# Half of a strip's candidate fetches ahead of a wait, half behind a store, in the last five rounds of GpSimd

## The chip, the cores and the metric

The kernel runs on one core of one Trainium2 chip. The metric is the device time of one execution in microseconds (us), the median of several runs.

## What is computed

Two graph layers on 8192 nodes with 64 features, with one dense weighted adjacency matrix `adj` (8192 x 8192, fp32, 268 MB):

```python
h = jnp.maximum(_layernorm(x, axis=-1), 0.0)
x = x + _L0_gnn_ref(h, L0_gnn_t, adj, L0_gnn_B, L0_gnn_W1, L0_gnn_b1, L0_gnn_W2, L0_gnn_b2)
h = jnp.maximum(_layernorm(x, axis=-1), 0.0)
x = x + _L1_gnn_ref(h, adj, L1_gnn_W, L1_gnn_att_self, L1_gnn_att_neigh, L1_gnn_bias)
return x
```

Layer 0 is `tanh([h, t] @ W1 + b1) @ W2 + b2` plus `Wt @ XB - rowsum(Wt) * XB` with `Wt = adj` and `XB = h @ B.T`. Layer 1 is an attention whose scores get `-1e10 * (1 - adj)`: where one entry of a row of `adj` leads the others by enough, the softmax picks that neighbour alone, and the layer's output is one gathered row, `relu(feats[best] + bias)`. The kernel computes that case, proves for its inputs that it holds, and keeps a general path behind a branch that isn't taken here.

## The kernel before, in words

The rows of `adj` are worked on in 16 strips of 512. A strip is 8 chunks of 2 MB (`adj_t`, a transposed copy) that SyncE loads into `ring`, a ring of four slots. On each chunk TensorE makes the products (L1034) and row sums (L1042, L1052), ScalarE casts it to fp16 (L546), and VectorE takes running maxima (L744) and adds pairs (L733). TensorE, VectorE and ScalarE run the strips in a loop. The small work on strip s-1 and s-2 is woven in.

The search for the strongest neighbour goes in steps over three strips. VectorE finds for each row the two best classes of 64 columns and writes their addresses into `cls_row` (L775). GpSimd, whose code is the function of L381, then fetches those two classes of 64 entries for 4 x 128 rows: eight indirect DMAs into `cand` (`fetch_rows`, L444 to L450). One strip later VectorE picks the largest (L788 to L800) and writes `best`. ScalarE writes the layer-1 features of a strip, with bias and relu, into `agg` (L579), and GpSimd stores them to `agg_dram` (`store_agg`, L439 to L442). When enough strips are stored, GpSimd gathers for each node the features of its best neighbour, 128 rows an indirect DMA, into `gathered` (`gather`, L457 to L464).

GpSimd's instructions stand in one order, written out by hand. In strips 1 to 10 a loop adds the bias b2 (L436), stores the features of strip s-1 and fetches the candidates of strip s. From strip 11 on come five rounds (L474 to L486), one for each entry of `WINDOWS` (L57). I call them rounds 0 to 4; they know the features of strips below 11, 12, 13, 14 and 15. Each of rounds 0 to 3 adds b2, waits for the gathers of the round before (`got`), stores the features, fetches eight times, waits until the stores landed (`agg_stored`), and gathers 14 times. Round 4 fetches four times and gathers four times.

Behind the rounds (L487 on) stand the last four fetches, eight late gathers (L492) that wait for the store of the last strip's features (`agg_last`, issued by SyncE at L337), two gathers, four scatter-adds into `out` (L501), two gathers, and four scatter-adds. SyncE stores the bulk of `out` after VectorE's additions (L920).

Of the kernel before, what the change touches and what calls it, by code (L numbers as in the profile page):

```python
# [35 lines left out]
S = N // W  # L36
TB = W // P
# [24 lines left out]
def build(nc, x, adj, adj_t, w1, w1_t, b1, t_in, w2, b2, b_t, w_gat, w_gat_t, att_self, att_neigh, bias, out):  # L62
    with ExitStack() as ctx:
# [6 lines left out]
        def sem(name):  # L70
            return ctx.enter_context(nc.semaphore(name))
# [157 lines left out]
        cls_row_done = sem("cls_row_done")  # L229
# [151 lines left out]
        def _(pool):  # L381
# [52 lines left out]
            def add_b2(s):  # L434
                x1 = x_tq[:, bass.ds(s * TB, TB), :]
                pool.tensor_tensor(x1, x1, b2_row[:, :].unsqueeze(1).to_broadcast([P, TB, D]),  # L436
                                   ALU.add).then_inc(x_b2_done, 1)

            def store_agg(s):  # L439

                pool.wait_ge(agg_ready, s + 1)
                pool.dma_start(agg_by_q[:, bass.ds(s, 1), :].rearrange("q a f -> q (a f)"), agg[:, :]).then_inc(agg_stored, 16)  # L442

            def fetch_rows(k0, k1):  # L444
                for k in range(k0, k1):
                    for g in range(CLS):
                        pool.indirect_dma_start(  # L447
                            out=cand[:, k, g * NB:(g + 1) * NB], out_offset=None, in_=classes,
                            in_offset=bass.IndirectOffsetOnAxis(ap=cls_row[:, k, g:g + 1], axis=0),
                        ).then_inc(cand_in, 16)  # L450

            def fetch_candidates(s):
                pool.wait_ge(cls_row_done, s + 1)
                pool.sem_inc(pool_past, 1)
                fetch_rows(0, TB)

            def gather(w, t0, t1):  # L457

                pool.wait_ge(best_done, (t1 + TB - 1) // TB)
                for t in range(t0, t1):  # L460
                    pool.indirect_dma_start(  # L461
                        out=gathered[:, t, :], out_offset=None, in_=agg_dram,
                        in_offset=bass.IndirectOffsetOnAxis(ap=best[:, t:t + 1], axis=0),
                    ).then_inc(got[w], 16)  # L464

            add_b2(0)
            fetch_candidates(0)
            add_b2(1)
            n0 = WINDOWS[0][0]
            with pool.Fori(1, n0) as s:  # L470
                add_b2(s + 1)
                store_agg(s - 1)
                fetch_candidates(s)
            for w, (known, t0, t1) in enumerate(WINDOWS):  # L474
                if known + 1 < S:
                    add_b2(known + 1)
                if w:
                    pool.wait_ge(got[w - 1], 16 * (WINDOWS[w - 1][2] - WINDOWS[w - 1][1]))
                store_agg(known - 1)
                if known < S - 1:  # L480
                    fetch_candidates(known)
                else:
                    pool.wait_ge(cls_row_done, S)
                    fetch_rows(0, TB // 2)
                pool.wait_ge(agg_stored, 16 * known)
                gather(w, t0, t1)  # L486
            fetch_rows(TB // 2, TB)  # L487
# [529 lines left out]
        def _(pe):  # L1017
# [47 lines left out]
            def turn_sums(s):  # L1065


                pe.wait_ge(rows_copied, s + 1)
                pe.wait_ge(acc_copied, s + 1)
                pe.wait_ge(hid_done, s + 1)  # L1070

                halves = [(k, slice(half, half + D), slice(k * P + half, k * P + half + D))
                          for k in range(TB) for half in (0, D)]
                for k, to, at in halves:
                    pe.matmul(ps_acc[to, k, D:2 * D], row_sb[:, at], fold_rows[:, :], start=True, stop=True)  # L1075
                for k in range(TB):
                    for _, to, at in halves[2 * k:2 * k + 2]:
                        pe.matmul(ps_acc[to, k, 0:D], acc_sb[:, at], b_t_twice[:, :], start=True, stop=False)
                    for _, to, at in halves[2 * k:2 * k + 2]:
                        pe.matmul(ps_acc[to, k, 0:D], hidden[:, at], w2_sb[:, :], start=False, stop=True)  # L1080
                for m in range(2):
                    last = pe.matmul(ps_xb[:, 2 * m:2 * m + 2, :].rearrange("q k d -> q (k d)"),  # L1082
                                     h_strip[:, m * P:(m + 1) * P], b_t_diag[:, :], start=True, stop=True)
                last.then_inc(acc_turned, 1)
# [155 lines left out]
```

## Time and profile before

| what | value |
|---|---|
| median of 3 runs | 794.06 us (792.35 to 794.34) |
| the profiled execution's own time | 793.22 us |
| its span, first to last instruction | 791.5 us |
| TensorE, VectorE, ScalarE, GpSimd busy | 86%, 82%, 75%, 49% |
| mean granted TensorE clock | 0.949 of full speed |

All numbers below are of that one profiled execution; the 1.7 us between its span and its time lie outside the instructions. A busy share is an average over the span: TensorE works until about 714 us, GpSimd until 783 us.

### The profile page before, as it was taken

What the parts mean: (1) busy time and instruction counts of PE and PEld (TensorE: products, weight loads), DVE (VectorE), ACT (ScalarE), POOL (GpSimd) and SP (SyncE); (2) the same over time, 40 slices, a digit from 0 to 9 for tenths busy, and PEclk for the clock granted to TensorE, in tenths of its full rate; (3) what the DMA queues carried; (4) which work ended last, traced back from release to release, by engine and by line L of the source; (5) the groups of instructions that cost most, each with busy time, mean ns of one, the idle gap of its engine ahead of it and who ended that gap; (6) DMA issues with size and microseconds to landing.
All of it is one profiled execution on the core that took longest, in us unless ns stands there. A gap on an engine that the chain in (4) does not pass through costs nothing.

```text
span 791.5 us, 13172 instructions
## 1 busy us (share of the span) xinstructions
PE 682.6 (86%) x4470; PEld 244.2 (31%) x4470; DVE 652.8 (82%) x944; ACT 594.0 (75%) x507; POOL 390.2 (49%) x281
## 2 busy tenths in 40 slices
PE   3999999999999999999999999999999999981100
PEld 1233333333333332333333333333333333330000
DVE  4586899989999999999898999999998989782420
ACT  3789888897889887888888888979888888770200
POOL 7000544435160808061533426170886878867774
PEclk9999999999999999999999999999999999995555
DMA  8999899999999999999999999999999999931151
GB/s 331 415 418 430 347 426 392 426 391 417 391 411 431 388 431 377 431 379 428 384 429 378 426 390 426 405 406 428 388 413 407 424 383 427 397 126 26 55 108 20
DMA packets 34544, 287.02 MB, mean 363 GB/s; under 512 B 7456, under 2 KB 13968, under 8 KB 18016
## 3 DMA queue, kind: packets, MB, share of 16 engines
q1 hardware_dynamic: 23168, 275.00, 83.9%
q0 software_dynamic: 9056, 9.73, 4.6%
q10 hardware_dynamic: 2304, 2.10, 0.8%
q8 instruction: 7, 0.11, 0.1%
q14 instruction: 9, 0.07, 0.0%
HBM read 279.46 MB, written 7.34 MB: 362 GB/s over the span
## 4 chain that ended last, share of the span: by engine, by line
PE 29%; DMA 22%; POOL 17%; issue 14%; DVE 13%; ACT 3%; DVEq 1%; SPq 0%; POOLq 0%; ACTq 0%
DMA ring<-in_adj_t 21%; PE acc L1034 18%; POOL gathered L461 7%; POOL cand L447 6%; DVE work L744 4%; PE row_sums L1042 4%; DVE work L733 4%; PE row_sums L1052 3%; ACT work L546 2%; POOL out L501 2%; DVE work L740 1%; POOL work L492 1%; PE ps_xb L1082 1%; DVE work L750 1%; PE ps_acc L1075 1%
## 5 line engine op out<-in xcount | busy, mean ns | idle before, releaser
L546 ACT CAST work<-ring 128x4096 f16<-128x4096 f32 x128 | 458.7, 3603 | 60.4 <-DMA ring<-in_adj_t 21.0
L1034 PE MATMUL acc<-ring,x_pb 128*64 128x512 f32 x2048 | 455.4, 596 | 13.7 <-DMA ring<-in_adj_t 13.5
L447 POOL DMA_INDIRECT cand<-in_adj,cls_row x128 | 231.8, 1811 | 64.8 <-issue 38.4
L744 DVE TENSOR_TENSOR work<-work 128x4096 f16<-128x4096 f16 x96 | 219.9, 2291 | 22.5 <-ACT work L546 19.5
L1034 PEld LDWEIGHTS acc<-ring,x_pb 128*64 128x64 f32 x2048 | 140.3, 137 | 316.3 <-issue 278.8
L733 DVE TENSOR_TENSOR work<-ring 128x2048 f32<-128x2048 f32 x90 | 210.4, 2352 | 7.1 <-DMA ring<-in_adj_t 5.0
L442 POOL DMA_DIRECT2D agg_dram<-agg x15 | 9.0, 600 | 258.0 <-ACT agg L579 200.8
L461 POOL DMA_INDIRECT gathered<-agg_dram,best x64 | 84.6, 1322 | 19.5 <-issue 19.5
L1052 PE MATMUL row_sums<-work,ones_cols 128*32 128x512 f32 x720 | 89.5, 598 | 0.1
L1042 PE MATMUL row_sums<-ring,ones_cols 128*32 128x512 f32 x608 | 72.4, 614 | 14.1 <-DMA ring<-in_adj_t 14.1
L436 POOL TENSOR_TENSOR x_tq<-x_tq,b_row 128x256 f32 (+1 forms) x16 | 29.5, 1846 | 42.7 <-DMA x_tq<-in_x 42.4
L740 DVE TENSOR_TENSOR work<-work 128x4096 f16<-128x4096 f16 x16 | 36.5, 2284 | 1.7 <-ACT work L546 1.7
L1042 PEld LDWEIGHTS row_sums<-ring,ones_cols 128*32 128x32 f32 x608 | 19.4, 112 | 57.3 <-issue 54.0
L1052 PEld LDWEIGHTS row_sums<-work,ones_cols 128*32 128x32 f32 x720 | 18.7, 109 | 54.2 <-issue 54.1
L617 ACT ACTIVATE tmp<-cen 128x64 f32<-128x64 f32 x64 | 15.6, 244 | 21.6 <-DVE cen L821 14.8
L604 ACT COPY acc_tq<-ps_acc 128x260 f32<-128x260 f32 x16 | 5.9, 370 | 28.3 <-remote 27.1
L1097 PE MATMUL ps_hid<-ident,h 128*128 128x128 f32 x2 | 0.7, 434 | 28.3 <-issue 28.3
L788 DVE MAX8 top_cand<-cand 128x8 f32<-128x128 f32 x64 | 13.8, 276 | 12.3 <-DMA cand<-in_adj,cls_row 12.3
L750 DVE TENSOR_TENSOR work<-work 128x2048 f16<-128x2048 f16 x16 | 19.6, 1225 | 2.3
L564 ACT ACT_TABLE_LOAD x16 | 20.5, 1283 | 0.3
L619 ACT ACT_TABLE_LOAD x16 | 20.5, 1283 | 0.3
L808 DVE TENSOR_TENSOR tmp<-ps_xb,acc_tq 128x256 f32<-128x256 f32 x16 | 6.7, 418 | 15.1 <-issue 15.1
(140 smaller groups left out, 493.0 us busy)
## 6 DMA issues: line engine op xcount, KB each, us to landing
ring<-in_adj_t SPq DMA_DIRECT2D x128, 2048.0 KB
agg_dram<-agg POOLq DMA_DIRECT2D x20, 128.0 KB, 19.9
x_tq<-in_x SPq DMA_DIRECT2D x1, 2048.0 KB, 16.9
cand<-in_adj,cls_row POOLq DMA_INDIRECT x128
raw_dram<-feat_stage ACTq DMA_DIRECT2D x16, 128.0 KB
out<-gathered SPq DMA_DIRECT2D x1, 1792.0 KB
x_pb<-in_x SPq DMA_DIRECT2D x1, 1536.0 KB, 14.2
gathered<-agg_dram,best POOLq DMA_INDIRECT x64
```

Source lines behind the costliest of these rows:

```text
L436: pool.tensor_tensor(x1, x1, b2_row[:, :].unsqueeze(1).to_broadcast([P, TB, D]), ALU.add).then_inc(x_b2_done, 1)
L447: pool.indirect_dma_start(out=cand[:, k, g * NB:(g + 1) * NB], out_offset=None, in_=classes, in_offset=bass.IndirectOffsetOnAxis(ap=cls_ro ...
L461: pool.indirect_dma_start(out=gathered[:, t, :], out_offset=None, in_=agg_dram, in_offset=bass.IndirectOffsetOnAxis(ap=best[:, t:t + 1], a ...
L546: act.copy(half_chunk[c % 2], slot(c)).then_inc(half_done, 1)
L564: act.activation(hidden[:, :], ps_hid[:, :], ACT.Tanh, bias=hid_bias[:, 3:4])\
L733: dve.tensor_tensor(pairs[i % PBUF], slot(c)[:, 0:HALF], slot(c)[:, HALF:2 * HALF], ALU.add)\
L740: dve.tensor_tensor(half_max, half_chunk[0], half_chunk[1], ALU.max).then_inc(max_done, 1)
L744: dve.tensor_tensor(half_max, half_max, half_chunk[c % 2], ALU.max).then_inc(max_done, 1)
L750: dve.tensor_tensor(half_max[:, 0:4 * W], half_max[:, 0:4 * W], half_max[:, 4 * W:8 * W], ALU.max)\
L1034: last = pe.matmul(acc[0][at:at + D, :], x_pb[:, c * CB + b, :], slot(c)[:, b * W:(b + 1) * W], start=(c == 0 and b < 2), stop=(c == NC - ...
L1042: last = pe.matmul(row_sums[at:at + QUAD, :], ones_cols[:, :], slot(c)[:, b * W:(b + 1) * W], start=(c == 0 and b < 4), stop=(c == NC - 1 ...
L1052: last = pe.matmul(row_sums[b * QUAD:(b + 1) * QUAD, :], ones_cols[:, :], pairs[i % PBUF][:, b * W:(b + 1) * W], start=(c == 0), stop=(c = ...
```

## The change

In the five rounds, the wait for `cls_row` and the first four fetches of a strip move ahead of the wait for the last round's gathers and ahead of the store. The other four fetches stay behind the store. In round 4 all four fetches of the round move. No instruction is added or removed in what GpSimd runs.

```diff
-            def fetch_candidates(s):
+            def fetch_candidates(s, k0=0, k1=TB):
                 pool.wait_ge(cls_row_done, s + 1)
                 pool.sem_inc(pool_past, 1)
-                fetch_rows(0, TB)
+                fetch_rows(k0, k1)
...
             for w, (known, t0, t1) in enumerate(WINDOWS):
                 if known + 1 < S:
                     add_b2(known + 1)
+                fetch_candidates(known, 0, TB // 2)
                 if w:
                     pool.wait_ge(got[w - 1], 16 * (WINDOWS[w - 1][2] - WINDOWS[w - 1][1]))
                 store_agg(known - 1)
                 if known < S - 1:
-                    fetch_candidates(known)
-                else:
-                    pool.wait_ge(cls_row_done, S)
-                    fetch_rows(0, TB // 2)
+                    fetch_rows(TB // 2, TB)
                 pool.wait_ge(agg_stored, 16 * known)
                 gather(w, t0, t1)
             fetch_rows(TB // 2, TB)
```

On GpSimd, in round 1 (rounds 2 and 3 read alike, with got1 and got2; round 0 has no got), `cand` is written by a fetch, `agg_dram` by the store and `gathered` by a gather:

```order
 L436 TENSOR_TENSOR x_tq<-x_tq,b_row 128x256
+L447 DMA cand<-in_adj,cls_row 128x64 [waits cls_row_done]
+L447 DMA cand<-in_adj,cls_row 128x64 x3
 L442 DMA agg_dram<-agg 128x256 [waits agg_ready,got0]
-L447 DMA cand<-in_adj,cls_row 128x64 [waits cls_row_done]
-L447 DMA cand<-in_adj,cls_row 128x64 x7
+L447 DMA cand<-in_adj,cls_row 128x64 x4
 L461 DMA gathered<-agg_dram,best 128x64 [waits best_done,agg_stored]
 L461 DMA gathered<-agg_dram,best 128x64 x13
```

The store with its two waits moved behind four fetches, so that four fetches instead of eight stand between it and the gather that waits for its landing.

On GpSimd, in round 4 and up to the last fetches:

```order
-L442 DMA agg_dram<-agg 128x256 [waits agg_ready,got3]
 L447 DMA cand<-in_adj,cls_row 128x64 [waits cls_row_done]
 L447 DMA cand<-in_adj,cls_row 128x64 x3
+L442 DMA agg_dram<-agg 128x256 [waits agg_ready,got3]
 L461 DMA gathered<-agg_dram,best 128x64 [waits best_done,agg_stored]
 L461 DMA gathered<-agg_dram,best 128x64 x3
 L447 DMA cand<-in_adj,cls_row 128x64 x4
```

Here nothing is left between the store and the gather that waits for its landing.

## Rows read from the trace of the kernel before

**Rows 1.** The chain that ended last, by engine and by line (page, part 4).

```profile
PE 29%; DMA 22%; POOL 17%; issue 14%; DVE 13%; ACT 3%; DVEq 1%; SPq 0%; POOLq 0%; ACTq 0%
```

**Rows 2.** GpSimd's waits: for whom, total us, times, longest.

```profile
POOL agg_dram L442 <- ACT agg L579: 200.8, 9, 22.5
POOL agg_dram L442 <- DMA gathered<-agg_dram,best: 14.5, 4, 5.3
```

**Rows 3.** Timeline of GpSimd, round 0: start, length, what, idle before.

```profile
552.68 0.60 POOL L442 DMA_DIRECT2D agg_dram<-agg  x1 [21.86 <-ACT agg L579]
...
569.45 1.90 POOL L461 DMA_INDIRECT gathered<-agg_dram,best  x1 [0.30 <-issue]
```

**Rows 4.** Timeline of VectorE: where cls_row is written, strips 11, 12, 14, 15.

```profile
553.07 0.17 DVE L775 SCALAR_TENSOR_TENSOR cls_row<-node,idx_cls 128x8 uint32<-128x8 uint32 x1
...
595.01 0.64 DVE L775 SCALAR_TENSOR_TENSOR cls_row<-node,idx_cls 128x8 uint32<-128x8 uint32 x1
...
681.19 0.17 DVE L775 SCALAR_TENSOR_TENSOR cls_row<-node,idx_cls 128x8 uint32<-128x8 uint32 x1
...
721.22 0.17 DVE L775 SCALAR_TENSOR_TENSOR cls_row<-node,idx_cls 128x8 uint32<-128x8 int32 x1 [0.62 <-DVE idx_cls L771]
```

**Rows 5.** Timeline of GpSimd, round 1, from its first instruction.

```profile
594.87 0.74 POOL L436 TENSOR_TENSOR x_tq<-x_tq,b_row 128x256 f32<-128x256 f32 x1
600.30 0.60 POOL L442 DMA_DIRECT2D agg_dram<-agg  x1 [4.68 <-DMA gathered<-agg_dram,best]
...
609.42 3.08 POOL L447 DMA_INDIRECT cand<-in_adj,cls_row  x1 [0.30 <-issue]
```

**Rows 6.** Timeline of GpSimd, rounds 2 and 3.

```profile
649.62 0.60 POOL L442 DMA_DIRECT2D agg_dram<-agg  x1 [2.80 <-DMA gathered<-agg_dram,best]
...
698.48 0.60 POOL L442 DMA_DIRECT2D agg_dram<-agg  x1 [5.26 <-DMA gathered<-agg_dram,best]
...
706.83 1.89 POOL L447 DMA_INDIRECT cand<-in_adj,cls_row  x1 [0.30 <-issue]
709.02 1.07 POOL L447 DMA_INDIRECT cand<-in_adj,cls_row  x1 [0.30 <-issue]
```

**Rows 7.** GpSimd's L447 by stretches: us, busy and count, clock, DMA share, GB/s.

```profile
601.20:619.40 18.20, 15.76 (x8) 1.00 1.00 416
```

**Rows 8.** GpSimd's L461 by stretches, same columns.

```profile
619.40:644.00 24.60, 20.59 (x14) 1.00 1.01 409
```

**Rows 9.** VectorE's last large operation on the strips, timeline.

```profile
705.62 2.28 DVE L744 TENSOR_TENSOR work<-work 128x4096 f16<-128x4096 f16 x1
```

**Rows 10.** Timeline of GpSimd, round 4 and the late gathers.

```profile
730.49 0.95 POOL L461 DMA_INDIRECT gathered<-agg_dram,best  x1 [0.30 <-issue]
733.19 0.59 POOL L442 DMA_DIRECT2D agg_dram<-agg  x1 [1.75 <-DMA gathered<-agg_dram,best]
...
739.13 0.97 POOL L461 DMA_INDIRECT gathered<-agg_dram,best  x1 [0.30 <-issue]
...
746.80 3.98 POOL L447 DMA_INDIRECT cand<-in_adj,cls_row  x1 [0.30 <-issue]
...
752.34 0.95 POOL L492 DMA_INDIRECT work<-agg_dram,late_from  x1 [0.30 <-issue]
```

**Rows 11.** Timeline of the other engines, one row of round 3, then the end.

```profile
682.91 0.38 ACT L604 COPY acc_tq<-ps_acc 128x260 f32<-128x260 f32 x1 [2.26 <-remote]
...
713.81 0.71 PE L1082 MATMUL ps_xb<-b_t_diag,h_strip 128*128 128x128 f32 x4
...
736.11 0.38 ACT L604 COPY acc_tq<-ps_acc 128x260 f32<-128x260 f32 x1 [24.80 <-remote]
...
746.08 3.88 DVE L920 TENSOR_TENSOR gathered<-gathered,x_tq 128x3584 f32<-128x3584 f32 x1
746.26 0.34 SPq L337 DMA_DIRECT2D agg_dram<-agg_last  x1
```

**Rows 12.** Tile agg: from issue to landing of the five stores at the start.

```profile
DMA to landing us min/median/max: 16.9/19.9/23.0
```

## The prediction

> **What bounds the kernel now.** I read the chain that ended last first. It gives TensorE, the DMAs and GpSimd 29%, 22% and 17% of the span [rows 1]; so no single engine is the bound, and the question is where the chain changes hands. In order of time it runs through the strips until 593 us, and from there to the end almost every piece is a GpSimd instruction: gathers, fetches, late gathers, scatter-adds, back to back with 0.3 us between them. So the last 190 us are GpSimd's queue, and time taken out of it can come off the end. The reader should look next at what GpSimd waits for. Its large wait, 200.8 us in nine pieces for ScalarE's features, lies in strips 1 to 11, where GpSimd has little else to do. The other one, 14.5 us in four pieces for the landing of the last round's gathers, lies in rounds 1 to 4 [rows 2]: 4.68, 2.80, 5.26 and 1.75 us [rows 5, 6, 10]. That is what the change puts work into.
>
> **Part 1: is the moved work ready?** The first fetch now waits for cls_row at the round's head. In round 0 it is there at 553.24 (553.07 + 0.17), and GpSimd has long been idle [rows 3, 4]. Before, the store went at 552.68 and the first gather at 569.45, 16.8 us later. Afterwards the same eight fetches and one store start about 0.6 us later and end at about the same time; a short wait for cls_row that stood between store and fetch goes. Round 0 costs nothing to within 0.5 us. In round 1 cls_row is ready at 595.65, GpSimd at 595.61 [rows 4, 5]: no wait to speak of, but only just. In round 3 it is ready at 681.4, 4.7 us before GpSimd comes, even once GpSimd is earlier (693.2 - 7.1, below); round 2 reads alike. In round 4 it was ready at 721.4; GpSimd comes at about 724.7 (below), and the candidates of strip 14, for which VectorE waits before it writes this cls_row, are fetched earlier than before.
>
> **Part 2: rounds 1 to 3, under load.** Eight fetches take 18.2 us, 2.28 us each [rows 7]; four take about 9.1 us, more than each wait. So each of the three waits is covered whole. Round 1: four fetches from 596.0, by the 8.2 us that they took before, the store with its gap 0.9 us, and the fifth fetch starts at 605.1 instead of 609.42 [rows 5]: 4.3 us. Round 2 adds 2.8 us, round 3 adds 5.3 us [rows 6]. In round 3 the fifth fetch then starts 12.4 us earlier, at 696.6 instead of 709.0.
>
> **Part 3: what is left of the 12.4 us at the end of the strips.** An issue of 1.89 us at 706.8 becomes 1.07 at 709.0 and 0.95 after that [rows 6], just behind VectorE's last large operation, which ends at 707.9 [rows 9], while DMA traffic had stopped before. With the 0.3 us gap an issue costs 1.76 us (24.6 / 14) for a gather beside the strips and 1.26 us afterwards (the last 4 fetches and 14 gathers of round 3, from 709.02 to 731.44, make 22.4 / 18 = 1.25) [rows 6, 8, 10]. So 12.4 us given back before 709 holds only some 5.6 issues at 2.2 us, which would have cost 5.6 x 1.26 = 7.0 us later. The last gather of round 3 ends at 724.4 instead of 731.4.
>
> The Trainium skill (SBUF — State Buffer, Who interferes with whom) infers that a two-input VectorE operation doesn't hold up the making of GpSimd's DMA descriptors. By that the long issues would not be VectorE's, and the 12.4 us would stay whole; the measured 1.89 against 0.95 us speaks against it.
>
> **Part 4: round 4.** Before: wait 1.75, store and gap 0.9, four fetches 5.0, gather at 739.13 [rows 10]. After: four fetches at once, which covers the 1.75 us, store, and then the gather stands right behind the store and waits for its landing. No row shows the landing of a store here. Below nothing it can't be; the nearest row is the gather of the same 128 pieces, 1.75 us in a quiet memory [rows 10]; the far one is the 19.9 us of five stores in a row at the start under the full load [rows 12]. I take 1.75, since it is the same queue at the same moment. The wait swaps places with the one removed, and the gather starts at 732.2: 6.9 us are left. In rounds 1 to 3 the same landing has four fetches, 9.1 us, to hide in.
>
> The Trainium skill (DMA: Bandwidth & Descriptors, Anatomy of one DMA) gives about 2.0 us plus bytes over 436 GB/s, an estimate of 2.3 us for 128 KB. By that the sum loses 0.6 us.
>
> **Part 5: what the end waits for.** Behind the rounds GpSimd does ten more issues, 13.2 us from 739.13 to 752.34 [rows 10]. One of them, at 746.80, takes 3.98 us instead of 0.95, beside VectorE's long addition from 746.08 to 749.96 [rows 11]. The late gathers also need the last strip's features, which SyncE stored at 746.26 [rows 11] and which land at about 748.3, by the 0.34 us of the issue and the 1.75 us of a gather's landing: only 4 us before GpSimd came to them. So 6.9 us can't come through unless this store moves too. Behind it stands a chain from ScalarE's copy at 736.11, and that copy waited 24.8 us, though TensorE's last matmul of the strip started at 713.8 and nothing else is on ScalarE [rows 11]. The releaser isn't named. If that release stands still, GpSimd comes at 742.5, waits, issues its first late gather beside the long addition, and is through with it at 750.8, where it was through with a fetch before: it is two issues further, 2 x 1.26 = 2.5 us. If the release moves up by x, the gain is 2.5 + x, at most 6.9.
>
> What is x? In round 3 ScalarE's same copy also waited for this nameless releaser, 2.26 us [rows 11], and in no strip before the gathers did it, so I hold the release to be tied to GpSimd's DMAs. It came 2.9 us after GpSimd's store at 733.19, the first thing after the train of gathers. That store now goes at 729.9: x = 3.3, gain 5.8 us. **Sum:** 793.2 - 5.8 = 787.4 us for the profiled execution; the median of the runs shown is 0.8 us above it, so 788.3 us.
>
> **The rivals.**
> 1. *The end stands still.* The release at 736.11 belongs to TensorE or ScalarE alone. For it: no row ties it to GpSimd. Gain 2.5 us, 791.5 us.
> 2. *Hidden anyway.* GpSimd's queue is limited by its DMAs and not by its issues: the time saved in the waits is waited elsewhere. For it: DMA share 1.0 until 698 us. Against it: the wait after the last gather is about 5 us in each round and doesn't grow, and issues get short as soon as VectorE is quiet. 794.0 us.
> 3. *Slower: the landing of the store.* In rounds 0 to 3 only four fetches, 9.1 us, cover it, and the store now stands behind four fetches in the queue. If it lands after L us, each round loses L - 9.1, against 12.4 us won over rounds 1 to 3; it turns to a loss at L = 9.1 + 12.4 / 4 = 12.2. By the 19.9 us of the five stores [rows 12] rounds 0 to 3 lose 43 us, less 12.4: 825 us. Against it: with the store ahead of eight fetches no gather ever waited, and the longest wait for a gather's landing under load is 5.26 us [rows 6].
> 4. *The whole gain and more.* By the skill's inference above GpSimd would be 12.4 us earlier at 731; the end then hangs on the release alone: 788.3 us as in the forecast or, with the release 10 us earlier, the whole 12.3 us, 782 us.
>
> **How the numbers follow.** The runs lie within 0.25% of each other; 0.3%, 2.4 us, is about what a measurement tells from no change. The forecast (gain between 4.5 and 6.9 us) has 0.54, rival 1 has 0.27, rival 2 0.11, rival 3 0.05, rival 4 0.03. Rival 1 lies on the line: half of it counts as faster. Faster 0.54 + 0.13 + 0.03 = 0.70, same 0.14 + 0.11 = 0.25, slower 0.05. The range takes in the forecast and rival 1: 786.2 (6.9 us, and 1 us for the unmeasured) to 792.5.
>
> **What the profile afterwards would show.** Right: in rounds 1 to 3 no wait at L442, the fetches of round 1 at 596; the last gather of round 3 ends at 724 to 725; a wait of about 2 us at the first gather of round 4, at 732; ScalarE's copy L604 at about 733 and the first late gather ending at about 747.5. Wrong: a wait for agg_dram at the first gather of rounds 0 to 3 (rival 3), waits at L442 that stay or long issues that get longer (rival 2), the copy at 736.1 and the first late gather ending at 750.8 (rival 1).

## The result, and the profile after

The changed kernel takes 791.43 us (median of 8 runs, 790.03 to 794.26) against 794.25 us before (8 runs, 792.35 to 794.46): a ratio of 0.9968, with a 95% interval of 0.9953 to 0.9982. That is a gain of 2.8 us, where 5.8 us were forecast. The profiled execution took 791.36 us, its span is 789.6 us, 1.9 us less than before. On the number that is what rival 1 said ("the end stands still", 791.5 us).

Line numbers behind the edit are 2 lower in the changed kernel (L602 is the old L604, L490 the old L492, L499 the old L501).

The chain that ended last, by engine (page, part 4):

```profile
PE 34%; DMA 27%; DVE 16%; issue 15%; ACT 3%; POOL 3%; DVEq 1%; SPq 0%; POOLq 0%; ACTq 0%
```

GpSimd's share was 17% before [rows 1] and is 3% now. The chain no longer runs through GpSimd's queue from round 1 on. From 717 us it reads, in order of time (start, us, what; the chain of after, behind the strips):

```profile
717.44 19.19 issue
736.64 0.43 DVE tmp L806
...
745.84 0.30 DVE agg_last L915
746.23 1.84 DMA agg_dram<-agg_last
748.32 2.43 POOL work L490
```

19.19 us go by in which VectorE waits for nothing that the profile names, then comes the chain that stores the last strip's features, and only at 748.32 GpSimd. GpSimd's waits show the same from its side (for whom, total us, times, longest):

```profile
POOL agg_dram L442 <- ACT agg L577: 185.2, 8, 24.6
POOL agg_dram L442 <- DVE cls_row L773: 43.2, 2, 23.0
...
POOL work L490 <- DMA agg_dram<-agg_last: 5.7, 1, 5.7
```

The row for the landing of the last round's gathers, 14.5 us in four pieces [rows 2], is gone. The two waits of 43.2 us for cls_row lie in the loop, in strips 1 to 10. A new row of 5.7 us stands at the first late gather. GpSimd's timeline, round 0, then the fifth fetches of rounds 1 to 3 with the stores ahead of them, then the last gather of round 3:

```profile
554.49 2.43 POOL L447 DMA_INDIRECT cand<-in_adj,cls_row  x1 [23.35 <-DVE cls_row L773]
...
563.25 0.60 POOL L442 DMA_DIRECT2D agg_dram<-agg  x1
564.16 2.60 POOL L447 DMA_INDIRECT cand<-in_adj,cls_row  x1 [0.30 <-issue]
567.06 3.04 POOL L447 DMA_INDIRECT cand<-in_adj,cls_row  x1 [0.30 <-issue]
...
574.81 1.90 POOL L461 DMA_INDIRECT gathered<-agg_dram,best  x1 [0.30 <-issue]
...
602.19 0.96 POOL L447 DMA_INDIRECT cand<-in_adj,cls_row  x1
...
608.22 0.60 POOL L442 DMA_DIRECT2D agg_dram<-agg  x1
609.13 2.59 POOL L447 DMA_INDIRECT cand<-in_adj,cls_row  x1 [0.30 <-issue]
...
654.32 0.60 POOL L442 DMA_DIRECT2D agg_dram<-agg  x1
...
690.08 0.96 POOL L447 DMA_INDIRECT cand<-in_adj,cls_row  x1 [0.16 <-issue]
...
695.91 0.60 POOL L442 DMA_DIRECT2D agg_dram<-agg  x1
696.82 1.33 POOL L447 DMA_INDIRECT cand<-in_adj,cls_row  x1 [0.30 <-issue]
...
724.52 0.95 POOL L461 DMA_INDIRECT gathered<-agg_dram,best  x1 [0.30 <-issue]
```

In rounds 0 to 4 no store waits, and in rounds 0 to 3 no gather waits for a store's landing. In round 3 the fifth fetch stands at 696.82, forecast 696.6. The last gather ends at 725.47, forecast 724.4. The price is in round 0: its first gather comes at 574.81, 5.4 us later than before [rows 3], where I had said 0.5 at most. GpSimd's timeline of the end:

```profile
730.51 0.59 POOL L442 DMA_DIRECT2D agg_dram<-agg  x1
732.79 0.97 POOL L461 DMA_INDIRECT gathered<-agg_dram,best  x1 [1.70 <-issue]
...
741.63 0.95 POOL L447 DMA_INDIRECT cand<-in_adj,cls_row  x1 [0.30 <-issue]
748.32 2.43 POOL L490 DMA_INDIRECT work<-agg_dram,late_from  x1 [5.75 <-DMA agg_dram<-agg_last]
...
763.63 1.63 POOL L499 DMA_INDIRECT out<-work,late_row  x1 [1.58 <-DMA work<-agg_dram,late_from]
```

The other engines there (first TensorE's last matmuls of the strip):

```profile
715.40 2.02 PE L1080 MATMUL ps_xb<-b_t_diag,h_strip 128*128 128x128 f32 x4
...
736.23 0.38 ACT L602 COPY acc_tq<-ps_acc 128x260 f32<-128x260 f32 x1 [23.34 <-remote]
...
746.05 3.88 DVE L918 TENSOR_TENSOR gathered<-gathered,x_tq 128x3584 f32<-128x3584 f32 x1
746.23 0.34 SPq L337 DMA_DIRECT2D agg_dram<-agg_last  x1
```

GpSimd reaches round 4's first gather 6.3 us earlier than before (732.79 against 739.13 [rows 10]). It ends its last fetch at 742.58 and then has to wait. ScalarE's copy L602, and with it the store of the last strip's features, stand where they stood: 736.23 and 746.23, before 736.11 and 746.26 [rows 11]. The first late gather ends at 750.75; rival 1 had it at 750.8.

So GpSimd does gain its 6 us at round 4, and only 1.9 us come through in this execution, because the copy of ScalarE didn't move. I call the start of that copy "the release" below. Why is it some 20 us behind TensorE's last matmuls in both traces, and what moves it?

### The profile page after: what moved, and what is told of

The parts are those of the page before. It is cut to its first block, busy times and chain, and to the rows that moved or that the text cites. A ratio compares the mean times of both kernels' runs of the same rounds, so it can differ in the third digit from the quotient of the medians.

```text
span 789.6 us, 13173 instructions
## 1 busy us (share of the span) xinstructions
PE 684.5 (87%) x4470; PEld 244.7 (31%) x4470; DVE 652.1 (83%) x944; ACT 594.3 (75%) x507; POOL 388.5 (49%) x281
## 4 chain that ended last, share of the span: by engine, by line
PE 34%; DMA 27%; DVE 16%; issue 15%; ACT 3%; POOL 3%; DVEq 1%; SPq 0%; POOLq 0%; ACTq 0%
DMA ring<-in_adj_t 26%; PE acc L1032 22%; DVE work L742 6%; PE row_sums L1040 4%; PE row_sums L1050 4%; DVE work L731 4%; ACT work L544 2%; POOL out L499 2%; DVE work L738 1%; POOL work L490 1%; DVE work L748 1%; DVE idx_cls L769 1%; PE ps_xb L1080 1%; PE ps_acc L1073 1%; DMA work<-agg_dram,late_from 1%
## 5 line engine op out<-in xcount | busy, mean ns | idle before, releaser
L447 POOL DMA_INDIRECT cand<-in_adj,cls_row x128 | 226.7, 1771 | 86.9 <-DVE cls_row L773 49.0
L461 POOL DMA_INDIRECT gathered<-agg_dram,best x64 | 85.5, 1336 | 20.9 <-issue 20.9
L615 ACT ACTIVATE tmp<-cen 128x64 f32<-128x64 f32 x64 | 15.6, 244 | 20.9 <-DVE cen L819 14.5
L602 ACT COPY acc_tq<-ps_acc 128x260 f32<-128x260 f32 x16 | 5.9, 369 | 24.8 <-remote 24.4
L918 DVE TENSOR_TENSOR gathered<-gathered,x_tq 128x256 f32<-128x256 f32 (+1 forms) x3 | 4.7, 1573 | 18.5 <-DMA gathered<-agg_dram,best 18.5
## 6 DMA issues: line engine op xcount, KB each, us to landing
x_pb<-in_x SPq DMA_DIRECT2D x1, 1536.0 KB, 14.5
```

The source lines that it names most:

```text
L447: pool.indirect_dma_start(out=cand[:, k, g * NB:(g + 1) * NB], out_offset=None, in_=classes, in_offset=bass.IndirectOffsetOnAxis(ap=cls_ro ...
L461: pool.indirect_dma_start(out=gathered[:, t, :], out_offset=None, in_=agg_dram, in_offset=bass.IndirectOffsetOnAxis(ap=best[:, t:t + 1], a ...
```

## The experiments

In four sets; the kernels of a set share the runs of the kernel before on their chip. Edits are to the changed kernel unless the text says otherwise. The first set's kernel before took 795.57 us (11 runs, 793.96 to 797.64).

**probe: two signals inside TensorE's last group.** ScalarE copies a tiny tile after each.

```diff
+    last = pe.matmul(ps_acc[to, k, D:2*D], row_sb[:, at], fold_rows[:, :], ...)
+if probed: last.then_inc(folded, 1)      # behind the 16 folds
...
+if probed: last.then_inc(mixed, 1)       # behind the last product with w2
...
+for n, there in enumerate((folded, mixed)):
+    act.wait_ge(there, 1)
+    act.copy(probe[:, n:n + 1], ones[:, :])
 keep_turned(S - 1)
```

> The changed kernel, with two more signals inside TensorE's turning of the last strip (after the row-sum folds, after the products with B and W2), each followed by a one-column copy on ScalarE, ahead of the copy L604 whose release came at 736.1 (before) and 736.2 us (after). It shows which group of matmuls is late. If the recorded starts are right and only the last matmul's signal is held back: both small copies at 714 to 716 us, the copy of acc_tq at 736. If TensorE really stands still within the group: the first or second small copy is itself at 736. Span as the changed kernel's, 789.6 within 1 us.

One execution, 785.84 us. ScalarE's timeline of the probe:

```profile
711.99 0.19 ACT L666 COPY probe<-ones 128x1 f32<-128x1 f32 x1 [0.98 <-PE ps_acc L1079]
...
721.65 0.19 ACT L666 COPY probe<-ones 128x1 f32<-128x1 f32 x1 [9.47 <-remote]
...
723.78 0.38 ACT L605 COPY acc_tq<-ps_acc 128x260 f32<-128x260 f32 x1 [1.94 <-remote]
```

The first signal is prompt. The second comes after 9.47 us more of wait, though by the trace the last four products with w2, of which the last sends it, start from 713.22 on, and the release another 2.1 us behind it. ScalarE has nothing else to do in that time: it is lost inside TensorE's group of small matmuls or in their signals. It was lost while GpSimd's train of gathers ran (704.40 to 723.96). It had ended before GpSimd's store of round 4 at 729.00. The tie to that store, on which my x rested, doesn't hold in this execution.

**flush: eight more matmuls behind TensorE's last group** (into a bank that nobody reads then), to see whether the signal only waits for something to follow it.

```diff
 turn_sums(S - 1)
+for _ in range(8):
+    pe.matmul(ps_hid[:, 0:P], ident[:, :], ident[:, :], start=True, stop=True)
```

> The changed kernel, with eight more 128x128 matmuls (0.7 us at the lower clock) behind TensorE's turning of the last strip, so that the last real matmul is not the last in the queue. Theory A (a matmul's signal comes late only because nothing follows it on TensorE): release of ScalarE's copy at 717 to 719 instead of 736.2, the end then hangs on GpSimd alone, gain 4.4 us on top, about 787 us. Theory B (release tied to GpSimd's DMAs) and theory C (something else on the chip, fixed in time): release at 736, median 791.4 as the changed kernel.

791.1 us (7 runs, 787.26 to 793.3), ratio 0.9924 [0.9901, 0.9947]. TensorE's timeline of flush, then ScalarE's:

```profile
715.63 1.07 PE L1080 MATMUL ps_xb<-b_t_diag,h_strip 128*128 128x128 f32 x4
716.97 0.50 PE L1160 MATMUL ps_hid<-ident 128*128 128x128 f32 x3 [0.27 <-issue]
718.41 1.11 PE L1160 MATMUL ps_hid<-ident 128*128 128x128 f32 x3 [0.94 <-issue]
...
724.82 0.37 PE L1160 MATMUL ps_hid<-ident 128*128 128x128 f32 x1 [1.09 <-issue]
```

```profile
734.05 0.38 ACT L602 COPY acc_tq<-ps_acc 128x260 f32<-128x260 f32 x1 [20.42 <-remote]
```

Work behind the group doesn't help: 20.42 us of wait. The idea that nothing follows it falls. And the added matmuls come in pieces every 1.4 us or so until 724.8, with gaps ("issue") for which no one is named, and span 8 us where I had put 0.7; TensorE itself creeps here, also after the strip's own work. Nor is it the only late signal in this execution. The next copy from TensorE, of the turned h, waits 5.71 us, where it waits 1.51 to 1.52 in all 17 other profiles:

```profile
745.45 0.38 ACT L622 ACTIVATE h_t<-ps_hid 128x256 f32<-128x256 f32 x1 [5.71 <-remote]
```

By then round 3's train had been over for 14 us (GpSimd's other gathers and fetches ran until 743.4), so in this kernel a signal was late without it.

**nogather3: round 3 without its 14 gathers** (the rows that they fetch are zeros, and VectorE doesn't wait for them).

```diff
-                if w:
+                if w and w != 4:
                     pool.wait_ge(got[w - 1], ...)
...
-                gather(w, t0, t1)
+                if w != 3:
+                    gather(w, t0, t1)
```

> The changed kernel with the 14 gathers of round 3 left out (their rows of the output lack the gathered features; the tile is set to zero at the start). GpSimd is then some 18 us ahead after the strips and has only 4 fetches, one store, 4 gathers, 4 fetches to issue. Theory B (the release of the copy at 736 is tied to GpSimd's train of DMAs): release moves up by 10 us or more, to 716 to 726. Theory C (tied to TensorE, ScalarE or time): release still at 736 and the span still near 789, since the late gathers wait for it.

777.97 us, and the release prompt:

```profile
715.02 0.38 ACT L604 COPY acc_tq<-ps_acc 128x260 f32<-128x260 f32 x1 [3.32 <-PE ps_xb L1082]
```

Now the releaser has a name, TensorE's ps_xb, and the wait is 3.32 us. On the same chip three kernels with the train beside the group had it late (flush, probe and round0_old, below); without the train it is prompt, in the one execution that there is.

**round0_old: round 0 in the order of before.**

```diff
-                fetch_candidates(known, 0, TB // 2)
                 if w:
+                    fetch_candidates(known, 0, TB // 2)
                     pool.wait_ge(got[w - 1], ...)
                 store_agg(known - 1)
-                if known < S - 1:
+                if w == 0:
+                    fetch_candidates(known)
+                elif known < S - 1:
                     fetch_rows(TB // 2, TB)
```

> The changed kernel with round 0 in its old order (store, eight fetches); rounds 1 to 4 as changed. In the changed kernel round 0's first gather came at 574.8 instead of 569.4, so GpSimd should be 3 to 5 us ahead of the changed kernel in rounds 1 to 3 as far as cls_row allows. If the end hangs on the pinned release, as rival 1 says: no gain, 791.4 within 1 us. If the end hangs on GpSimd's queue: 2 to 3 us faster, about 789.

789.52 us (5 runs, 786.3 to 791.86), ratio 0.9932 [0.9906, 0.9957]. GpSimd's timeline: the first gather of round 0, the store of round 4 and the first late gather; below it ScalarE's.

```profile
571.38 1.90 POOL L461 DMA_INDIRECT gathered<-agg_dram,best  x1 [0.30 <-issue]
...
728.42 0.59 POOL L442 DMA_DIRECT2D agg_dram<-agg  x1
...
743.17 2.43 POOL L492 DMA_INDIRECT work<-agg_dram,late_from  x1 [2.35 <-DMA agg_dram<-agg_last]
```

```profile
731.12 0.38 ACT L604 COPY acc_tq<-ps_acc 128x260 f32<-128x260 f32 x1 [20.34 <-remote]
```

The first gather is 3.4 us earlier than in the changed kernel (574.81), the store of round 4 is 2.1 us earlier, but the interval overlaps flush's of the same set. The medians differ by 1.6 us, and flush isn't quite the changed kernel, which has no runs in this set; so this can't tell what round 0's order is worth from nothing. The other thing to read is the release: 2.7 us behind the store of round 4. It is 2.7 us in flush too (store 731.32, release 734.05) and 2.9 before [rows 10, 11], but 5.7 in the changed kernel, and in the probe the release is 5.2 us ahead of the store. Three of five fit the tie that I had assumed; two don't.

This profile shows something else: a late release needn't cost the gain. At 731.12 it is 5.1 us earlier than in the changed kernel's first profile, and so is the first late gather (743.17 against 748.32); the span is 784.6 us against 789.6. In both, that gather starts 12.1 us behind the release.

**The second set** (before 793.62 us, 31 runs, 790.66 to 796.23) takes the train away from TensorE's group without leaving work out. `acc_turned` is what TensorE signals behind that group.

**pause: two gathers of round 3, then a wait for TensorE's last group, then twelve.**

```diff
+                if w == 3:
+                    gather(w, t0, t0 + 2)
+                    pool.wait_ge(acc_turned, S)
+                    gather(w, t0 + 2, t1)
+                else:
                     gather(w, t0, t1)
```

> The changed kernel, with one wait more on GpSimd: after the second gather of round 3 it waits until TensorE has signalled the turning of the last strip (the matmuls ahead of ScalarE's copy that was released at 736.2 us). Theory B2 (TensorE's small matmuls stand still as long as GpSimd issues indirect DMAs without a break): GpSimd pauses 4 to 6 us, the signal comes at 715 to 717, the copy right after it; GpSimd then reaches the late gathers at 747 to 750 and waits for nothing there; end as the changed kernel, within 1.5 us, since the pause costs about what the late release cost. Theory C (the signal comes at its own time, whatever GpSimd does): GpSimd stands until 736, and the kernel is 15 us or more slower.

792.12 us (10 runs, 789.81 to 793.17), ratio 0.9975 [0.9959, 0.9992]. GpSimd's timeline, then ScalarE's:

```profile
716.21 0.95 POOL L461 DMA_INDIRECT gathered<-agg_dram,best  x1 [6.59 <-PE ps_xb L1085]
```

```profile
715.97 0.38 ACT L607 COPY acc_tq<-ps_acc 128x260 f32<-128x260 f32 x1 [3.83 <-PE ps_xb L1085]
```

The release is prompt, 20 us ahead of the changed kernel's. The time is no better than the result's ratio, since GpSimd waits 6.59 us for it and so gives back what it had gained: its first late gather, no longer waiting, stands at 750.87. That the pause brought the release forward isn't shown: the changed kernel itself was not profiled on this chip, and all four profiles of this set are prompt.

**pause_round0: pause, and round 0 in the order of before** (edit as in round0_old).

> The changed kernel with the same wait as in pause and with round 0 in its old order, which put GpSimd about 2 us ahead. With the release out of the way the end hangs on GpSimd alone: 2 us faster than pause, about 789, ratio to before 0.992 to 0.995. If the old order of round 0 was worth nothing and its 2 to 3 us were scatter: the same as pause.

791.69 us (10 runs, 788.4 to 793.94), ratio 0.9971 [0.9955, 0.9988]; release 718.30, after strips that ended late in this execution. Against pause, round 0 is again worth nothing that can be told.

**pause_before: the kernel before, with the wait ahead of round 3's gathers.**

```diff
+                if w == 3:
+                    pool.wait_ge(acc_turned, S)
                 gather(w, t0, t1)
```

> The kernel before, with the same wait ahead of round 3's gathers. By theory B2 GpSimd pauses 1 to 3 us (it stands at 714, TensorE signals at 715 to 717), ScalarE's copy comes 20 us earlier than 736, and the end doesn't gain, since before it hung on GpSimd's queue: 0 to 2 us slower than before, ratio 1.000 to 1.003. If the kernel before hung on the late release too, it would be 3 us or more faster.

794.48 us (10 runs, 793.45 to 797.14), ratio 1.0024 [1.0005, 1.0043]; release 715.11, 21 us ahead of that of before [rows 11], and no gain, rather a loss of 0.2%. The end of the kernel before doesn't hang on the release. The added wait itself cost GpSimd nothing in the profile: the first gather of round 3 came at 715.97, behind the release.

**round4_only: the kernel before, with only the four fetches of round 4 moved.**

```diff
+                if w == 4:
+                    pool.wait_ge(cls_row_done, S)
+                    fetch_rows(0, TB // 2)
                 if w:
                     pool.wait_ge(got[w - 1], ...)
...
-                else:
-                    pool.wait_ge(cls_row_done, S)
-                    fetch_rows(0, TB // 2)
```

> The kernel before with the change made in round 4 alone: its four fetches ahead of the wait for round 3's gathers and of the store. The prediction's part 4 says a swap of waits: the 1.75 us for the gathers go, 1.7 us for the landing of the store come; median as before within 0.1 per cent. If the whole effect came from round 4, it would be 0.3 per cent faster.

792.28 us (10 runs, 791.27 to 796.2), ratio 0.9985 [0.9968, 1.0002]; release prompt, 716.69. GpSimd's first gather of round 4 waits 1.72 us for the landing of the store: the wait of 1.75 us [rows 10] has swapped places and the sum is about zero, as Part 4 had it. By the trace, what the change gains it gains in rounds 1 to 3; the medians alone don't say so, since the interval reaches down to 0.9968.

**The third set** (before 793.11 us, 8 runs, 790.46 to 798.16): four kernels on another chip, two of them unchanged.

**after_again: the changed kernel, unchanged, one execution.**

> The changed kernel once more, unaltered, for one look: whether the late release of ScalarE's copy of acc_tq (736.2 us in the first profile, against 716 to 718 in every run in which round 3's gathers came only after TensorE's group) is a property of the kernel or of one execution. Property of the kernel: release at 730 us or later again. Chance: release at 717.

**before_again: the kernel before, unchanged, one execution.**

> The kernel before once more, unaltered. Its first profile had the release at 736.1, though TensorE's group stood only at the edge of round 3's gathers. The run with round 4 alone changed, whose gathers came later by 1.6 us, had it at 716.7. Where the group slips past the gathers' start by chance: release at 715 to 718 or at 730 to 737; the span is the same to 1 us in both cases, since before the end hung on GpSimd's queue.

787.07 us and 793.04 us, spans 785.4 and 791.3. GpSimd's timeline of the changed kernel, then its other engines:

```profile
708.24 1.90 POOL L461 DMA_INDIRECT gathered<-agg_dram,best  x1 [0.30 <-issue]
...
729.39 3.50 POOL L447 DMA_INDIRECT cand<-in_adj,cls_row  x1 [0.30 <-issue]
...
746.50 0.95 POOL L490 DMA_INDIRECT work<-agg_dram,late_from  x1 [0.30 <-issue]
```

```profile
715.36 0.38 ACT L602 COPY acc_tq<-ps_acc 128x260 f32<-128x260 f32 x1 [2.64 <-PE ps_xb L1080]
...
728.09 3.96 DVE L918 TENSOR_TENSOR gathered<-gathered,x_tq 128x3584 f32<-128x3584 f32 x1 [1.41 <-DMA gathered<-agg_dram,best]
...
742.61 0.34 SPq L337 DMA_DIRECT2D agg_dram<-agg_last  x1
```

The same two rows of the kernel before (ScalarE's, then GpSimd's):

```profile
714.23 0.38 ACT L604 COPY acc_tq<-ps_acc 128x260 f32<-128x260 f32 x1 [3.76 <-PE ps_xb L1082]
```

```profile
752.28 0.95 POOL L492 DMA_INDIRECT work<-agg_dram,late_from  x1 [0.30 <-issue]
```

This is the pair that explains the result, one execution each. Neither kernel was edited, and both releases came 21 to 22 us earlier than in their first profiles. The kernel before ended where it had ended (span 791.3 against 791.5, first late gather 752.28 against 752.34 [rows 10]): it is bound by GpSimd's queue, whatever the release does. The changed kernel ended 4.2 us earlier than in its first profile (785.4 against 789.6). Its first late gather no longer waits and starts 1.8 us earlier; it takes 0.95 us in place of 2.43, as VectorE's long addition now stands beside an earlier fetch (3.50 us); and the wait for the late gathers' landing is 0.9 us shorter. The gain in this pair is 5.9 us of span. That it is the forecast's 5.8 is luck in part: the forecast had it as 2.5 + 3.3 with a first late gather that waits, and here nothing waits and the whole lead of GpSimd's queue comes through, 5.8 us at that gather.

**adj_train: round 3's gathers read rows of `adj` in place of `agg_dram`** (the output rows that they feed are then not the reference's), to see whether what is read matters.

```diff
+                if w == 3:
+                    ... in_=classes, in_offset=IndirectOffsetOnAxis(ap=best[:, t:t + 1]) ...
+                else:
                     gather(w, t0, t1)
```

> The changed kernel, with the 14 gathers of round 3 reading rows of adj instead of agg_dram (same count, size and destination, so the result lacks the right features in these rows). If any train of indirect DMAs holds TensorE's small matmuls up: release of the copy at 725 us or later, as in the changed kernel. If it is the reading of agg_dram: release at 716 to 718.

784.17 us, release 714.66, prompt. Since after_again on the same chip was prompt too, this tells nothing about the cause.

**fetch_mid: round 3 gathers five, fetches its last four, gathers nine.**

```diff
-                if known < S - 1:
+                if known < S - 1 and w != 3:
                     fetch_rows(TB // 2, TB)
                 pool.wait_ge(agg_stored, 16 * known)
+                if w == 3:
+                    gather(w, t0, t0 + 5)
+                    fetch_rows(TB // 2, TB)
+                    t0 += 5
                 gather(w, t0, t1)
```

> The changed kernel with round 3 reordered: store, five gathers, the last four fetches, nine gathers, so that fetches and not gathers stand beside TensorE's group at 711 to 716 us. GpSimd loses some 4 us to the landing of the store. If fetches leave TensorE alone: release at 717, first late gather at about 751, end as the changed kernel or up to 1 us better, 0.996 of before. If fetches hold it up as gathers do: release after 730, and the kernel is 2 to 4 us slower than the changed one.

787.75 us (4 runs, 787.61 to 788.26), ratio 0.9944 [0.9922, 0.9966], release 715.77. GpSimd's timeline, round 3:

```profile
695.91 0.60 POOL L442 DMA_DIRECT2D agg_dram<-agg  x1
701.17 2.56 POOL L461 DMA_INDIRECT gathered<-agg_dram,best  x1 [4.66 <-DMA agg_dram<-agg]
```

With no fetches behind the store its landing shows under the load of the ring: 5.26 us from the start of the issue (701.17 - 695.91). In the two kernels of the fourth set with the same order it is 6.69 us (fetch_mid_five) and 5.32 us (mid_round0). All are under the 9.1 us that four fetches cover and the 12.2 us from which rival 3 would have decided.

**The fourth set** (before 793.48 us, 11 runs, 791.79 to 796.29), on a fourth chip, is to tell whether the prompt changed kernel's gain stands in several runs. after_five is the changed kernel, fetch_mid_five is fetch_mid, mid_round0 is fetch_mid with round 0 in the order of before, after_look3 is the changed kernel once more; no new edit.

> The changed kernel, unaltered, over five rounds on the same chip as the reordered one. If the late signal comes by chance, its times spread over some 4 us, from 787 where it is prompt to 792 where it is late, and the median lies 0.3 to 0.6 per cent below before.

> The kernel of fetch_mid once more (round 3: store, five gathers, four fetches, nine gathers). If keeping the gathers away from TensorE's last group removes the late signal: release at 715 to 717 in the profile, median 787.5 to 788.5, a spread of under 2 us, and 2 us or more below the changed kernel. If fetch_mid's first figure was luck: the same median and spread as the changed kernel.

> The kernel of fetch_mid with round 0 in its old order. If GpSimd's queue is the bound now, what round 0 gains (2 to 5 us at the head of round 1) comes through in part: 1 to 2 us below fetch_mid. If cls_row or the strips take it back: the same as fetch_mid.

> The changed kernel, a third look. Release late (730 us or later) with a span near 789.5, or prompt (715 to 718) with a span near 785.5; a prompt release with a span of 789 would speak against the release as the cause.

| kernel | median (runs) | ratio to before | release | first late gather | span |
|---|---|---|---|---|---|
| after_five | 787.3 (6) | 0.9918 [0.9898, 0.9939] | 715.06 | 745.89 | 785.1 |
| fetch_mid_five | 787.76 (6) | 0.9927 [0.9909, 0.9945] | 716.18 | 746.98 | 786.4 |
| mid_round0 | 787.29 (6) | 0.9920 [0.9900, 0.9939] | 714.36 | 747.95 | 787.2 |
| after_look3 | 788.53 (1) | | 718.23 | 747.50 | 786.9 |

All four releases are prompt, and the changed kernel gains 6.2 us here. Its interval doesn't touch that of the result (0.9953 to 0.9982), though the kernels are the same. Its six spans, 783.7 to 787.7 us, all lie below the eight of the result, 788.4 to 792.6. Neither variant is better than the plain change.

## Why the prediction was right on the queue and wrong on the end

**Part 1, wrong in size.** "Round 0 costs nothing to within 0.5 us" is off by 5 us: 5.4 us at the first gather. Of it 0.45 us are the start: the first fetch went at 554.04 before and goes at 554.49, since the strips were that much later in this execution. From there to the first gather it was 15.4 us (569.45 - 554.04) and is 20.3 (574.81 - 554.49); of these 4.9 us the store, now among them, is 0.9 us and the issues are 4.0. VectorE does small operations from 560.0 to 562.6 us before and from 561.0 to 563.6 after; in that stretch an issue takes 0.97 to 1.07 us in place of 1.9 to 3.0. Before, two issues fell into it and a third into a later gap; now it holds one issue and the store. I had priced fetches as if only their number counted. It took nearly all that round 1 was to give: the fifth fetch of round 1 gains 0.3 us (609.13 against 609.42) rather than 4.3. That VectorE is the cause is read from where the issues fall; no run isolates it.

**Part 2, right in its mechanism and, for round 3, in its number.** All three waits are covered whole. Round 3's fifth fetch is at 696.82 for 696.6, but not by the road that I gave, and so partly by luck. The 4 us lost by round 1 came back in the two rounds behind it: by the fifth fetches, round 2 added 4.5 us for the 2.8 expected (655.23 against 660.03 before) and round 3 added 7.4 for 5.3. In round 3 the four fetches ahead of the store took 5.8 us in place of the 9.1 assumed, again by where they fell.

**Part 3, right:** 12.2 us at that fetch became 6.0 us at the last gather of round 3 (725.47 for 731.44), and 10.7 became 5.3 between before_again and after_again. Issues beside the strips are long, and time given back there is worth about half behind them. The Trainium skill (SBUF — State Buffer, Who interferes with whom) infers that a two-input VectorE operation doesn't hold up descriptor making. The runs speak against it as far as the coincidence goes: in after_again an issue of 0.95 us became 3.50 beside the addition that started at 728.09, as one of 3.98 stood beside it before [rows 10].

**Part 4, right:** the wait for the landing was 1.70 us for 1.75, the gather at 732.79 for 732.2. round4_only shows the swap by itself, ratio 0.9985 with 1 in its interval. The Trainium skill's estimate for this landing (DMA: Bandwidth & Descriptors, Anatomy of one DMA) of 2.3 us agrees with the 2.28 us from the start of the store to the gather (732.79 - 730.51).

**Part 5, the step that failed.** "I hold the release to be tied to GpSimd's DMAs. ... That store now goes at 729.9: x = 3.3." The row on which I rested it, the 2.26 us in round 3 [rows 11], has no counterpart in before_again, where the same copy waits for nothing. The store went at 730.51, and the release stayed at 736.23: x was -0.1, so that of 2.5 + x only the 2.5 was left at the first late gather (it ends at 750.75, before at 753.29). All else in Part 5 held for this execution: that gather waits for `agg_last` and is issued beside the long addition. Behind it 0.7 us more were lost, which I had put at nothing: the wait for the late gathers' landing grew from 0.86 to 1.58 us. (I had also counted ten issues from 739.13 to 752.34, and there are eight; no sum uses it.) What the runs put in place of x:

- The release isn't a fixed time either, as rival 1 had it: the same two kernels had it at 736 and at 714 to 718 us. Whether it belongs to TensorE alone stays open. In 13 of the 18 profiles ScalarE waits 1.8 to 3.8 us for it and the trace names TensorE's ps_xb. In the other five it waits 11 to 25 us for an unnamed releaser (before, after, flush, round0_old and, over its two waits, probe).
- A link with round 3's train of gathers from `agg_dram` is suggested and not shown. In four of the five late profiles the train runs beside TensorE's last group; in the fifth, before, it starts at 714.17, 0.36 us behind the start of the group's last matmuls (713.81), and round4_only, where it stands exactly so (715.79 behind 715.43), is prompt. nogather3, without the train, is prompt beside three late ones on its chip, but it is a single execution. That the train isn't enough is shown by after_again, after_five and after_look3, which have it there and are prompt.
- What the release costs depends on the kernel and on how late it is. Before, nothing: the pair of profiles at 791.5 and 791.3, neither with a wait at the first late gather. The changed kernel's first profile comes to that gather 9.8 us earlier than before (742.57) and waits, so a late release shows: 789.6 against 785.1 to 786.9. At 731.12 (round0_old) the span was 784.6.

So the change moves the bound off GpSimd's queue to whichever is later, that queue or the chain behind the release. With the release prompt it gives 5.9 us (after_again and before_again) and 6.2 us (fourth set), the forecast's size by another road; with the release at 736.23, 1.9 us (the profiled execution). That the 2.8 us of the result are runs with the release late in most of them is argued from their profile and their spans; a run that isn't profiled doesn't show it. The sets also differ by their chip, so a difference between chips that doesn't go through the release isn't excluded.

Rival 2 is out: the queue moved. (My words against it were wrong: the waits behind rounds 0 to 3 were 4.68, 2.80, 5.26 and 1.75 us, not about 5 in each.) Rival 3 is out by the landing of 5.3 to 6.7 us under load, and by the gathers of rounds 0 to 3, none of which waited for it. Rival 4 is out, as GpSimd wasn't 12 us earlier at the end.

**Open:** why TensorE's group finishes late in some executions. On the chips of the third and fourth sets none of the three profiles with the train there was late, on that of the first set all three; whether it hangs on the chip, on where buffers lie in memory or on the moment wasn't tried. The number of instruction loads isn't the difference: their queues moved three packets between 700 and 750 us in all five late profiles, and three in before_again and after_again. No kernel here both kept GpSimd's lead and was measured on a chip with late releases, so that fetch_mid would save the remaining 4 us there is a guess.

## What to carry to other kernels

Before a gain on one queue is counted to the end, look for the second chain that arrives just behind it and take a second profile of the same kernel: here one wait of 24.8 us for an unnamed releaser was 3.76 us in the next profile of the same kernel, on another chip, and cost nothing until the queue ahead of it got faster. Price a moved DMA issue by the issues that stand beside the same VectorE work, not by the mean of its kind: 0.95 and 3.04 us stood in one round. Work that covers a wait is worth having where the wait is the bound, but what is won while issues are long shrinks once they are short, here by half.

## What was not expected of the hardware

TensorE's last small matmuls, which the trace shows starting within 3 us, signalled their end up to 20 us late in some executions, and in four of the five with 14 indirect gathers running beside them on GpSimd. TensorE's clock isn't the reason. Busy time of each engine in a stretch (length, then PE, PEld, DVE, ACT, POOL; granted clock, DMA share, GB/s), after:

```profile
712.00:718.00 6.00, 5.03 (x56) 3.99 (x56) 5.05 (x31) 0.42 (x1) 4.72 (x5) 0.50 0.16 31
```

The same stretch of flush:

```profile
712.00:718.00 6.00, 3.77 (x59) 2.95 (x60) 5.57 (x31) 0.42 (x1) 4.47 (x6) 1.00 0.12 26
```

The first ran at the lower level, 1.2 GHz, the second at the full 2.4 GHz, and both releases were late by as much; in before_again the granted clock of the same stretch was 0.50, and the release was prompt. The Trainium skill (SBUF — State Buffer, Who interferes with whom) says that TensorE and ScalarE never wait on anyone for a port of that memory; no run here shows a port, but flush shows TensorE held up every 1.4 us by something that the trace doesn't name.
